# Building the linking matrices of a graph kernel: both masks from one two-byte comparison, counts by a two-byte product, weights by a four-byte product of half the width

## What is computed

```python
def _L0_gnn_ref(x, edge_index, W1, b1, W2, b2):
    row, col = (edge_index[0], edge_index[1])
    summed = jax.ops.segment_sum(x[col], row, num_segments=n)
    deg = jax.ops.segment_sum(jnp.ones((row.shape[0],), x.dtype), row, num_segments=n)
    agg = summed / jnp.maximum(deg, 1.0)[:, None]
    ...
def _L2_gnn_ref(emb, vals, rows, cols):      # vals = edge_weight, rows = src, cols = dst
    gathered = vals[:, None] * x[cols]
    side = jax.ops.segment_sum(gathered, rows, num_segments=n)
    light_out = (emb + 3 * side) / 4
```

## Time and profile before

| | us |
|---|---|
| median of 3 runs (5418.67 to 5431.08) | 5429.41 |
| the profiled execution | 5436.53 |
| its span | 5434.8 |

### The profile page before, as it was taken

How to read it: one execution, slowest core, us unless ns; L and a number is a source line. 1 busy time by engine, 2 the same in 40 slices (tenths; PEclk the granted TensorE clock), 3 DMA queues, 4 the chain that set the end, 5 groups by cost and what they waited for, 6 DMA issues and landing times. The chain is left out here.

```text
span 5434.8 us, 50013 instructions
## 1 busy us (share of the span) xinstructions
PE 3062.4 (56%) x13750; PEld 2237.6 (41%) x13751; DVE 2231.2 (41%) x2709; ACT 614.3 (11%) x1076; POOL 3413.0 (63%) x3213
## 2 busy tenths in 40 slices
PE   3899989567777777744918633343333333333333
PEld 1788879233333333324917422232222323232223
DVE  7999985445555454568901331111111111101112
ACT  0455540000000000004701000000000000000000
POOL 2888868466556555657770356666666666666664
PEclk7999999666666666657958766665665656555555
DMA  5566667144444444425825332222222111111111
GB/s 177 157 181 192 177 198 230 37 131 138 132 133 139 132 135 130 139 87 159 259 62 195 136 100 70 69 64 60 60 59 60 48 46 46 45 46 46 46 46 46
DMA packets 498663, 599.91 MB, mean 110 GB/s; under 512 B 190115, under 2 KB 367441, under 8 KB 496248
## 3 DMA queue, kind: packets, MB, share of 16 engines
q0 software_dynamic: 117856, 246.12, 16.5%
q1 hardware_dynamic: 337751, 229.77, 14.8%
q10 hardware_dynamic: 42944, 122.68, 6.0%
HBM read 406.69 MB, written 204.36 MB: 112 GB/s over the span
## 5 line engine op out<-in xcount | busy, mean ns | idle before, releaser
L720 POOL DMA_INDIRECT rec_by_src<-rec,pos x782 | 1123.3, 1436 | 524.6 <-issue 238.9
L1132 PE MATMUL ps<-g_got,g_hot 128*128 x3224 | 687.5, 367 | 1225.8 <-issue 797.4
L1132 PEld LDWEIGHTS ps<-g_got,g_hot 128*128 128x128 f32 x3224 | 605.7, 272 | 1320.2 <-issue 1318.9
L1592 POOL DMA_INDIRECT sc_kv<-kv,d_src x806 | 761.8, 945 | 533.9 <-DVE sc_kve L1644 260.2
L1032 POOL DMA_INDIRECT g_got<-y_forward,d_msg x782 | 739.3, 945 | 381.8 <-issue 230.1
L1032 POOL DMA_INDIRECT g_got<-y_back,s_msg x782 | 737.8, 943 | 381.2 <-issue 233.5
L805 PE MATMUL ps<-ln_low,ln_hot 128*125 128x256 f32 x2848 | 620.3, 381 | 20.3 <-DVE ln_low L782 16.1
L805 PEld LDWEIGHTS ps<-ln_low,ln_hot 128*125 128x125 f32 x2848 | 535.6, 188 | 104.8 <-issue 24.4
L1043 DVE TENSOR_TENSOR g_hot<-ps,src_loc 128x1024 f32<-128x1024 f32 x101 | 120.6, 1221 | 992.5 <-remote 450.4
L1699 PE MATMUL ps<-w_e,sc_attrT 128*128 128x512 f32 x404 | 320.0, 887 | 246.0 <-ACT sc_attrT L1611 216.3
L1051 DVE TENSOR_TENSOR g_y<-ps,ms_b 128x384 f32<-128x384 f32 x75 | 41.8, 558 | 808.8 <-remote 474.2
(11 more groups left out here) (323 smaller groups left out, 3283.7 us busy)
## 6 DMA issues: line engine op xcount, KB each, us to landing
linked<-ln_out SPq DMA_DIRECT2D x320, 224.0 KB
ve<-sc_kve ACTq DMA_DIRECT2D x202, 256.0 KB
wv_ve<-ve SPq DMA_DIRECT2D x101, 512.0 KB
l_links<-linked SPq DMA_DIRECT2D x25, 800.0 KB
l_links<-linked ACTq DMA_DIRECT2D x25, 800.0 KB
f_links<-linked SPq DMA_DIRECT2D x25, 800.0 KB
f_links<-linked ACTq DMA_DIRECT2D x25, 800.0 KB
attr_pairs<-ln_feats POOLq DMA_DIRECT2D x7, 2048.0 KB
```

The costliest lines, as they stand in the source:

```text
L720: pool.indirect_dma_start(out=dram["rec_by_src"], out_offset=bass.IndirectOffsetOnAxis(ap=S["pos"][:, c:c + 1], axis=0), in_=S["rec"][:, c ...
L1132: last = pe.matmul(ps[:, bass.ds(columns[j], width)], hot[:, q, j, :], got[:, bass.ds(slots[j], width)], start=False, stop=True, skip_grou ...
L1592: pool.indirect_dma_start(out=kv[:, q, j, :], out_offset=None, in_=dram["kv"], in_offset=bass.IndirectOffsetOnAxis(ap=S["d_src"][:, c:c + ...
```

## The change

One comparison now makes both kinds of marks, in bf16. `index_stage` writes `low` and `key` in turn, every number twice, into one bf16 array `win_twice` (for pair c: low, low, key, key), and `ln_short` is a bf16 copy of the column numbers, made once before the loop. With pairs of equal numbers the comparison reads every operand by two adjacent bf16 values: 16 rows of 64 pairs. Its result `ln_marks` has for each pair of the staircase 128 marks of `low` and 128 of `key`. VectorE then multiplies the `low` marks with the f32 weights into `ln_heavy` (f32, 8x128), behind a wait for the comparison, and casts the 8x125 `key` marks to f32 in `ln_hot`.

TensorE makes two products for each pair in place of one: `ln_hot` with `ln_heavy` in f32 (128 columns, weights), and the bf16 `key` marks with the bf16 `low` marks (128 columns, counts). Offsets are loaded for two groups at once, and the loops step over pairs of groups.

```diff
 # index_stage, ScalarE
-                act.activation(array[:, :], turn_of(n, s.cols), ACT.Copy).then_inc(kept, 1)
+                if what in TWICE:
+                    act.activation(array[:, :].rearrange("p (c k t) -> p c k t", k=2, t=2)[:, :, TWICE.index(what), :],
+                                   turn_of(n, s.cols).unsqueeze(2).to_broadcast([P, s.cols, 2]), ACT.Copy).then_inc(kept, 1)
+                else:
+                    act.activation(array[:, :], turn_of(n, s.cols), ACT.Copy).then_inc(kept, 1)
 # link_nodes, VectorE
+            dve.tensor_copy(short[:, :], S["col"][:, :]).then_inc(shortened, 1)
+            dve.wait_ge(shortened, 1)
             def group(i, q):
-                cols = bass.ds(i * (W_WAYS * GROUP) + q * GROUP, GROUP)
+                start = i * (W_WAYS * GROUP) + q * GROUP
+                numbers = S["win_twice"][:, bass.ds(start * 4, 4 * GROUP)].rearrange("p (c t) -> p c t", t=2)
+                by_pair = marks[:, q].rearrange("p (c k) n -> p c k n", k=2)
                 dve.wait_ge(paired, i * W_WAYS + q + 1)
-                dve.tensor_tensor(low[:, q, :, 0:P], S["col"][:, :].unsqueeze(1).to_broadcast([P, GROUP, P]),
-                                  S["win_lo"][:, cols].unsqueeze(2).to_broadcast([P, GROUP, P]), ALU.is_equal).then_inc(marked, 1)
-                dve.tensor_tensor(hot[:, q], S["col"][:, 0:KEYS].unsqueeze(1).to_broadcast([P, GROUP, KEYS]),
-                                  S["win_key"][:, cols].unsqueeze(2).to_broadcast([P, GROUP, KEYS]), ALU.is_equal).then_inc(heated[q], 1)
+                dve.tensor_tensor(marks[:, q].rearrange("p c (n t) -> p c n t", t=2),
+                                  short[:, :].rearrange("p (n t) -> p n t", t=2).unsqueeze(1).to_broadcast([P, 2 * GROUP, P // 2, 2]),
+                                  numbers.unsqueeze(2).to_broadcast([P, 2 * GROUP, P // 2, 2]), ALU.is_equal).then_inc(marked, 1)
                 dve.wait_ge(marked, i * W_WAYS + q + 1)
-                dve.tensor_tensor(low[:, q, :, P:2 * P], low[:, q, :, 0:P],
-                                  S["win_w"][:, cols].unsqueeze(2).to_broadcast([P, GROUP, P]), ALU.mult).then_inc(heated[q], 1)
+                dve.tensor_tensor(heavy[:, q], by_pair[:, :, 0, :],
+                                  S["win_w"][:, bass.ds(start, GROUP)].unsqueeze(2).to_broadcast([P, GROUP, P]), ALU.mult).then_inc(heated[q], 1)
+                dve.tensor_copy(hot[:, q], by_pair[:, :, 1, 0:KEYS]).then_inc(heated[q], 1)
 # link_nodes, TensorE
-            def group(i, q):
+            def two_groups(i, q):
                 start = i * (W_WAYS * GROUP) + q * GROUP
                 _, slots = nc.values_load_multi_w_load_instructions(
-                    steps[0:1, bass.ds(start, GROUP)], engines=[mybir.EngineType.PE], min_val=0,
+                    steps[0:1, bass.ds(start, 2 * GROUP)], engines=[mybir.EngineType.PE], min_val=0,
...
+                for k in range(2):
+                    group(i, q + k, slots[k * GROUP:(k + 1) * GROUP])
...
                 for j in range(GROUP):
-                    last = pe.matmul(ps[0:KEYS, bass.ds(slots[j], 2 * P)], hot[:, q, j, :], low[:, q, j, :],
+                    pe.matmul(weights[:, bass.ds(slots[j], P)], hot[:, q, j, :], heavy[:, q, j, :],
+                              start=False, stop=True, skip_group_check=True)
+                    last = pe.matmul(counts[:, bass.ds(slots[j], P)], marks[:, q, 2 * j + 1, 0:KEYS], marks[:, q, 2 * j, :],
                                      start=False, stop=True, skip_group_check=True)
```

More of the change, by code:

```diff
@@ L72 @@
 BANK = 512
+TWICE = ("low", "key")
 assert 2 * GROUP * (RING - 4) >= BLOCKS - 1 + GROUP and PAIRS_PAD % 24 == 0 and PAIRS_PAD + 2 * GROUP <= PAIR_COLS and BLOCKS % CHUNK == 0 and TILES % (2 * SCAT) == 0
@@ L736, in link_nodes @@
     MAIN = KEYS // 16 * 16
+    assert REST % 2 == 0
     with ExitStack() as stack:
         m = Memory(nc, stack)
+        marks = m.sb("ln_marks", [P, W_WAYS, 2 * GROUP, P], BF16)
         hot = m.sb("ln_hot", [P, W_WAYS, GROUP, KEYS])
-        low = m.sb("ln_low", [P, W_WAYS, GROUP, 2 * P])
+        heavy = m.sb("ln_heavy", [P, W_WAYS, GROUP, P])
+        short = m.sb("ln_short", [P, P], BF16)
         out = m.sb("ln_out", [P, REGIONS, REGION])
@@ L744, in link_nodes @@
         brought, laid = m.sem("ln_brought"), m.sem("ln_laid")
-        paired, cleared, blank, marked = (m.sem("ln_" + n) for n in ("paired", "cleared", "blank", "marked"))
+        paired, cleared, blank, marked, shortened = (m.sem("ln_" + n) for n in ("paired", "cleared", "blank", "marked", "shortened"))
         heated = [m.sem(f"ln_heated{q}") for q in range(W_WAYS)]
@@ L809, in _ @@
             with pe.Fori(0, WHOLE) as i:
-                for q in range(W_WAYS):
-                    group(i, q)
-            for q in range(REST):
-                group(WHOLE, q)
+                for q in range(0, W_WAYS, 2):
+                    two_groups(i, q)
+            for q in range(0, REST, 2):
+                two_groups(WHOLE, q)
         @block.scalar
@@ L2251, in gnn_kernel @@
                 sort_by_block(nc, S, dram)
-                S["win_key"], S["win_lo"], S["win_w"] = (j.sb("win_" + n, [P, W_COLS]) for n in ("key", "lo", "w"))
+                S["win_twice"], S["win_w"] = j.sb("win_twice", [P, W_COLS * 4], BF16), j.sb("win_w", [P, W_COLS])
                 S["win_steps"] = j.sb("win_steps", [1, (2 * W_BLOCKS + SPLIT_BLOCKS) * P], I32)
@@ L2255, in gnn_kernel @@
                 index_stage(nc, S, dram, "ix", 1, dram["rec_by_dst"],
-                            [("win", NODES, W_BLOCKS, [(S["win_lo"], "low"), (S["win_key"], "key"), (S["win_w"], "weight")]),
+                            [("win", NODES, W_BLOCKS, [(S["win_twice"], "low"), (S["win_twice"], "key"), (S["win_w"], "weight")]),
                              ("dst", P, PAIR_BLOCKS, [(S["dst_loc"], "local"), (S["d_src"], "source")], True)],
```

3 lines of the change are left out of this document (added).

## The result

The changed kernel takes 5891.4 us (median; 5887.5 to 5894.7) where the kernel before takes 5430.2 (5418.7 to 5443.7): a ratio of 1.0848, 95% interval 1.0821 to 1.0874. It is slower by 461 us; 5353 was forecast. The profiled execution took 5894.7 us, its span is 5893.0.

The account below looks back on a forecast made before the run. VectorE and TensorE were taken to bound the linking stage; VectorE's 3.08 us a group over 178 groups, 548 us, brought the next stage 76.5 us earlier: 5353 us forecast, its own range 5339 to 5375, wider range 5320 to 5430.

Parts of the forecast that it names:

- VectorE's terms: Linking loop: comparison to product 1.30, product 1.14, cast 0.59, sends' delays 0.05; 3.08 us a group.
- Rivals C and D: VectorE's cast at one a cycle, 5446 us, chance 0.06; its comparison not packed, 2.29 us, 5543 us, chance 0.12.
- TensorE's array: Linking loop: 16 f32 and 8 bf16 passes a group, 1.78 to 2.67 us, 2.7 taken, under VectorE's 3.08.
- TensorE's sequencer: Linking loop: issuing, address steps and register loads bounded at up to 4.1 us a group, taken as below 3.08.
- Rival B: TensorE's sequencer bounds the linking loop: 3.4 us a group gives 5410 us, 3.5 gives 5428; chance 0.12.
- GpSimd was priced as harmless: Linking stage: two sends a group, 1.54 us each, done at 628, before VectorE's end at 698.2.
- Clock: TensorE idles some 0.4 us in each 3.1 us; a lower granted clock was priced at nothing.
- the range to 5430: Total time of 5320 to 5430 us, holding the forecast and three rivals, chance 0.82.

Follow-up runs that it names:

- e8: Changed kernel, offsets loaded per group and only 2 of 8, all pairs added into the first's window (sums wrong): 3.05 us a group.
- e7: Changed kernel with 8 offsets a load, limit's load and wait moved from TensorE to VectorE: 5775.6 us, ratio 1.0640 (kernel before at 5433.6).
- e6: Changed kernel, GpSimd's sends tied to TensorE's progress, 8 offsets loaded per group instead of 16 for two: 4749.6 us, ratio 1.0203.
- e4: Kernel before, VectorE's three instructions a group replaced by two of eight elements (masks zero): 4662 us beside 4655.
- e3: Changed kernel with GpSimd's sends in the linking stage tied to TensorE's progress: 4758.9 us, ratio 1.0224.
- e17: Changed kernel with only GpSimd's sends tied to the matmuls, a repeat: 4760.0 us beside 4657.2, ratio 1.0223.
- e18: Changed kernel itself, unedited, in a set where the kernel before takes 4657.2 us: 4757.6 us, ratio 1.0216.
- e13: Kernel before, VectorE's three large instructions replaced by two of eight elements, where the kernel before takes 5430.9 us: 5814.1 us.
- e14: Changed kernel with 8 offsets a load, limit on VectorE, sends tied to the matmuls: 5389.9 us beside 5430.9, ratio 0.9929.

## Why the prediction was wrong

**VectorE's terms** were right, each of them. The comparison is packed (1.224 us), the cast runs at two a cycle (0.673), the product starts 1.34 us after the comparison (1.30 was taken), and where nothing holds VectorE the group takes 3.05 us (e8). The wait costs 0.04 more than the earlier trace rows gave. The sum was 3.08. Rivals C and D are refuted. The Trainium skill, Vector Engine (DVE) Microarchitecture Reference, section 5.1, has a row read again and again, with two sources, in packed mode, and two elements as enough for it; the 1.224 us agrees.

**TensorE's array** was right too: 24 passes take 2.62 us (eight pairs 0.33 us apart), for 2.7.

**TensorE's sequencer is the step that failed first:** the prediction took its period to be below VectorE's 3.08 us, and it was 3.93. The working had its terms in hand: 48 instructions and 16 address steps, and then "0.39 to 0.77 + 0.30" for the loads. Issuing was right: at 0.03 an instruction plus 0.037 an address step it is 2.03 us; 1.93 was measured (600 to 1200 us of after). The term for everything around it was 0.69 to 1.07 and is 2.00: the load of 16 offsets 1.53 us, so 0.76 a group; the limit 0.35; and 0.9 for the register steps, the assertion and the waits after each load, which I had not counted because each is 0.02 to 0.15 us long, with as much between them. 1.93 + 2.00 = 3.93, as the windows gave. e7 and e8 took some of it away, and the period fell with it; e6 only divided it otherwise and got nothing. Rival B was thus the case, and its 3.4 to 3.5 us too low. I set it aside because in the row I calibrated on the earlier trace rows "the array itself could be the limit". That was a reason for a lower bound, not for choosing it; the range given in the same paragraph reached 4.1.

Why before did not suffer: its sequencer has 8 address steps and 16 instructions fewer to issue, behind an array that takes 3.5 us a group, and e4 shows that array full. The change took 0.9 us of array work out of a group and put 8 address steps with their matmuls in, some 0.12 us each by the 1.93 for 16, so 1 us of issuing. This alone made the kernel 2.2% slower in the second sort (e3, e17), which would have been outside the range.

**GpSimd was priced as harmless**, and this is the larger error. The text had "with the port free one send comes every 1.27 us" and counted it as a gain, sends done at 628. Where the stage goes undisturbed the last came near that, at 605 in e18, but by luck: a group took 4.2 us there and not 3.08, and a send came every 1.43 us and not every 1.54. What I didn't ask is what a GpSimd that never pauses does to others. A trace of before could have warned. In the gather stages after 2700 us, where VectorE hardly works, TensorE's instructions stand 0.70 and 1.40 us apart in places under the name "issue":

```profile
4799.94 0.29 PEld L1132 LDWEIGHTS ps<-g_got,g_hot 128*128 128x128 f32 x1 [1.81 <-issue]
4800.65 0.37 PE L1132 MATMUL ps<-g_got,g_hot 128*128 x1 [1.02 <-issue]
4801.35 0.29 PEld L1132 LDWEIGHTS ps<-g_got,g_hot 128*128 128x128 f32 x1 [1.12 <-issue]
4802.05 0.37 PE L1132 MATMUL ps<-g_got,g_hot 128*128 x1 [1.03 <-issue]
```

I looked at no row there, since the change didn't touch those stages. The order of events in after fits the theory: the pace leaves VectorE idle (first for 0.7 us up to 175.2), the sends close up to 1.27 us, and at 181 the first matmuls are late. But that is order and not proof; the proof that unpaced sends beside an idle VectorE bring the stretch on, in the first sort, is e13, and e7 against e14.

**Clock** was priced at nothing. In the pace of after it is 0.93 and the f32 matmul's mean 320 ns, with e7's 302 at 1.00; since the sequencer is the bound, that cost little. In the slow stretch it is 0.50, beside an array that is busy 18 of 150 us.

**The chances.** All cases were about one stage's VectorE or TensorE alone; the range to 5430 had no case in which two engines disturb each other, and none for a stage in which the engine relieved had been what held a third one back.

**What stays open.** What the slow issue is. SyncE suffers as well, so it isn't the array or its clock alone. Nor do the instructions seem to be brought in late: the Trainium skill, Runtime: NRT & Kernel Launch, section Instruction fetch mechanics, says that fetching runs ahead and is mostly hidden, and that a taken branch out of the part held forces a stall. The rows at 353 to 357 lie in the midst of a group, with no branch among them, and are late all the same. And between 190 and 580 us, where TensorE makes 162 matmuls, the DMA queues bring two packets of kind "instruction":

```profile
q14 instruction: 2, 0.02, 0.0%
```

Open too is why some sets show it and others not. So is what else it takes beside sends without a pause: in e13 they had come every 1.27 us for 35 us before the first late matmul, and in the gather stages of before 41 matmuls take 7.57 us from 4802.75 on, though GpSimd sends every 1.25 us from 4803.54. Between which intervals of the sends it starts wasn't tried (1.27 us shows it, 1.75 doesn't). After the last send of the stage TensorE stays slow for another 22 us, in after (564.3 to 586.5) and in e13 (555.1 to 576.8), so the sends' own time on GpSimd can't be all of it.

## What to carry to other kernels

Before halving an array's work, add up its sequencer's whole period, from the first address step of one round to that of the next, small register steps and waits included; in this kernel they were half of it. If the engine you relieve shares something with a third one, ask what that third one does once it is free, and look in the same trace for a place where it is free already. Work that has slack is better tied to the progress of the bound engine than left to run ahead: in one sort of sets that turned 1.064 into 0.993 here, and in the other it cost nothing that shows (e18 and e17).

## What the runs showed of the hardware

- Beside indirect transfers of GpSimd sent every 1.27 us, and for 22 us after the last, TensorE's instructions came 0.70 or 1.40 us apart and SyncE's issues took 2.6 instead of 0.65 us (2.62 for four at 707.92), in three sets of runs and never in three others; sent every 1.75 us, they did no such harm (e14: 3.26 us a group, and 3.27 in e7 after its last send).
- The same kernel before takes 5430 or 4655 us by the set, 17% apart, so a time means something only beside its own set's. The steps of 0.70 and 1.40 us show with the first of the two alone; whether they are the whole of the 17% wasn't tried.
- A load of registers on TensorE from a tile in SBUF took at least 0.30 us for one, 0.59 for eight and 1.10 for sixteen values, with medians up to 0.96 (eight, e7) and 1.52 (sixteen). The Trainium skill, DMA: Bandwidth & Descriptors, section Latency and other measured facts, has a floor of about 600 ns for such a load; the 0.30 us of one value is below it.
- A bf16 pass of 128 columns with its weights between f32 passes costs TensorE the same 0.11 us as an f32 one: three passes a pair, 0.33 us (600.81 to 601.14 in after, at the full clock).
